# First attention of a two-layer graph transformer: the order of its loads and stores on the SyncE queue

## The reference

```python
x0 = layernorm(x)
for l in range(2):
    q = ((x0 @ Wq[l].T + bq[l]) * scaling).reshape(n, H, DH)
    k = (x0 @ Wk[l].T).reshape(n, H, DH)
    v = (x0 @ Wv[l].T).reshape(n, H, DH)
    scores = einsum('ehd,ehd->eh', q[tgt], k[srcidx])       # one score per edge and head
    w = softmax of scores over the edges that end in one node
    agg = segment_sum(w[:, :, None] * v[srcidx], tgt)
    x0 = batchnorm(x0 + agg @ Wo[l].T + bo[l])
    x0 = batchnorm(x0 + relu(x0 @ W1[l].T + b1[l]) @ W2[l].T + b2[l])
x = x + layernorm(x0)
x = x + small three-way MLP on decoded features of layernorm(x)
```

## Time and profile before

| | us |
|---|---|
| runs: median of 3 (lowest, highest) | 1113.53 (1112.64, 1302.58) |
| the profiled execution, its own time | 1110.29 |
| its span, first to last instruction | 1108.5 |
| PE busy in it | 1024.0 (92%) |
| DVE busy | 763.8 (69%) |
| ACT busy | 597.0 (54%) |
| POOL busy | 304.4 (27%) |
| PE waiting in the key jobs of layer 0 for VectorE | 3.67 |
| PE waiting in the first attention for `q_stack` | 3.61 |

### The profile page before, as it was taken

How to read it: one execution, slowest core, us unless ns; L and a number is a source line. 1 busy time by engine, 2 the same in 40 slices (tenths; PEclk the granted TensorE clock), 3 DMA queues, 4 the chain that set the end, 5 groups by cost and what they waited for, 6 DMA issues and landing times. The chain is left out here.

```text
span 1108.5 us, 18755 instructions
## 1 busy us (share of the span) xinstructions
PE 1024.0 (92%) x6579; PEld 852.7 (77%) x6579; DVE 763.8 (69%) x2350; ACT 597.0 (54%) x1096; POOL 304.4 (27%) x312
## 2 busy tenths in 40 slices
PE   4899899987999999999899999899999999989853
PEld 3678777876888888888699889788888888869842
DVE  6777647556777777777488730577777777747787
ACT  6633322435666666666425542566666666652366
POOL 1000000004444444443022200244444444421404
PEclk9999999999999999999999999999999999999985
DMA  6042310758112112113302454731211211320403
GB/s 146 24 158 79 116 46 23 165 136 217 41 35 58 38 38 62 38 38 112 114 1 99 105 127 102 179 65 38 61 38 38 62 38 39 112 86 1 94 4 93
DMA packets 50718, 84.98 MB, mean 77 GB/s; under 512 B 15190, under 2 KB 33466, under 8 KB 50372
## 3 DMA queue, kind: packets, MB, share of 16 engines
q1 hardware_dynamic: 50628, 83.82, 30.2%
HBM read 36.50 MB, written 21.61 MB: 52 GB/s over the span
## 5 line engine op out<-in xcount | busy, mean ns | idle before, releaser
L1259 POOL TENSOR_SCALAR probs<-probs,mass_inv 125x1250 f32<-125x1250 f32 x160 | 210.6, 1316 | 341.8 <-DVE mass_inv L1384 341.8
L1375 DVE CUSTOM_DVE_ANT_0 probs<-banks,scores_bias 125x416 f32<-125x416 f32 (+1 forms) x480 | 267.2, 582 | 49.6 <-PE banks L1279 45.2
L1279 PE MATMUL banks<-k_stack,q_stack 128*125 128x416 f32 (+1 forms) x960 | 294.7, 392 | 5.8 <-DMA q_stack<-q_split 3.6
L1293 PE MATMUL banks<-ident,probs 125*125 125x125 f32 x1600 | 258.6, 276 | 8.1 <-DVE probs_t L1366 5.8
L1293 PEld LDWEIGHTS banks<-ident,probs 125*125 125x125 f32 x1600 | 240.4, 187 | 32.0 <-issue 22.3
L1345 ACT ACTIVATE probs<-probs,neg_peak 125x1250 f32<-125x1250 f32 x160 | 213.4, 1334 | 54.4 <-DVE neg_peak L1398 54.4
L1334 ACT ACTIVATE probs_t<-banks 125x500 f32<-125x500 f32 x320 | 152.3, 477 | 111.9 <-PE banks L1293 111.9
L1308 PE MATMUL banks<-probs_t,v_pair 125*64 125x250 f32 x1600 | 186.2, 379 | 0.9 <-ACT probs_t L1334 0.9
L1279 PEld LDWEIGHTS banks<-k_stack,q_stack 128*125 128x125 f32 x960 | 143.8, 188 | 34.1 <-issue 15.9
L1308 PEld LDWEIGHTS banks<-probs_t,v_pair 125*64 125x64 f32 x1600 | 107.5, 136 | 54.3 <-ACT probs_t L1334 1.3
L1366 DVE COPY probs_t<-banks 125x500 f32<-125x500 f32 x160 | 108.1, 675 | 54.6 <-PE banks L1293 54.6
(11 more groups left out here) (256 smaller groups left out, 1410.3 us busy)
## 6 DMA issues: line engine op xcount, KB each, us to landing
q_stack<-q_split SPq DMA_DIRECT2D x160, 125.0 KB, 2.3
scores_bias<-edge_bias SPq DMA_DIRECT2D x8, 1171.9 KB
edge_bias<-bias_row SPq DMA_DIRECT2D x10, 585.9 KB
k_stack<-k_lo SPq DMA_DIRECT2D x16, 312.5 KB, 4.3
resid<-residual SPq DMA_DIRECT2D x2, 2500.0 KB, 9.7
values<-v_stage SPq DMA_DIRECT2D x2, 2400.0 KB
residual<-t SPq DMA_DIRECT2D x4, 625.0 KB, 3.0
xs<-in_x SPq DMA_DIRECT2D x5, 480.0 KB
```

The lines of the kernel that those rows point to most:

```text
L1259: nc.gpsimd.tensor_scalar(probs[:, u % 4, :], probs[:, u % 4, :], mass_inv[:, u % 4:u % 4 + 1], 1.0, ALU.mult, ALU.mult).then_inc(att["pro ...
L1279: mm = nc.tensor.matmul(pb[0:NT, t % 5, 0:sn], q_stack[:, n % 2, half, part, tile * NT:(tile + 1) * NT], k_stack[:, head * N + s0:head * N ...
L1293: mm = nc.tensor.transpose(pb[0:NT, 5 + t % 2, j * NT:(j + 1) * NT], probs[:, u % 4, (j0 + j) * NT:(j0 + j + 1) * NT], ident[0:NT, 0:NT])
L1375: nc.vector.tensor_tensor_reduce(out=probs[:, slot % 4, s0:s0 + sn], in0=pb[0:NT, t % 5, 0:sn], in1=scores_bias[:, (n % GROUPS) * GROUP + ...
```

## The change

It reorders what SyncE issues around the start of the first attention. `next_bias` is parted in `second_bias` (row 3) and `third_bias` (rows 4 and 5), and `values_out` in two parts, tiles 0 to 2 and tiles 3 to 9, with a semaphore each. In the first layer the store of the last bias row now stands right behind `first_bias`, ahead of the loads of rows 3 to 5; `k_stacked` of chunks 0 and 1 stand ahead of the queries of pass 1, with row 3 between them; rows 4 and 5 and the first part of the values are issued in the attention block. In both layers `stacked(2)` stands ahead of the load of rows 6 and 7, `stacked(3)` ahead of rows 8 and 9, and SyncE waits for the values ahead of `stacked(5)` instead of `stacked(4)`. ScalarE waits for the first part of the values before result 0 and for the second before result 5. No instruction of TensorE, VectorE, ScalarE or GpSimd is added, taken away or moved.

```diff
--- before.py
+++ after.py
@@ -240,7 +240,7 @@
 
         proj = {k: sem("p_" + k) for k in ("wq", "wv", "vec", "bias_q", "filled", "hi", "done", "copied")}
         k_stored = [sem("k_stored0"), sem("k_stored1")]
-        v_stored = sem("v_stored")
+        v_stored = [sem("v_stored0"), sem("v_stored1")]
         bias_in = [sem(f"bias_in{g}") for g in range(GROUPS)]
         v_in = [sem("v_in0"), sem("v_in1")]
         q_in = [sem("q_in0"), sem("q_in1")]
@@ -401,10 +401,14 @@
                 cols = slice((2 * c + half) * N, (2 * c + half + 1) * N)
                 sp.dma_start(f32(k_stack[other, cols]), f32(k_lo[c % 2][own, :])).then_inc(k_stored[c % 2], 16)
 
-        def values_out(sp):
+        V_PARTS = (slice(0, 3), slice(3, TILES))
+
+        def values_out(sp, k):
+
+            tiles = V_PARTS[k]
 
             for rows in SPREAD:
-                sp.dma_start(v_d.rearrange("(t p) d -> p t d", p=NT)[rows, :, :], v_stage[rows, :, :]).then_inc(v_stored, 16)
+                sp.dma_start(v_d.rearrange("(t p) d -> p t d", p=NT)[rows, tiles, :], v_stage[rows, tiles, :]).then_inc(v_stored[k], 16)
 
         def first_bias(sp):
 
@@ -414,11 +418,15 @@
             for rows in SPREAD:
                 sp.dma_start(scores_bias[rows, GROUP:GROUP + 1, :], bv[rows, GROUP:GROUP + 1, :]).then_inc(bias_in[1], 16)
 
-        def next_bias(sp):
+        def second_bias(sp):
 
             bv = bias_d.rearrange("(t p) s -> p t s", p=NT)
             for rows in SPREAD:
                 sp.dma_start(scores_bias[rows, GROUP + 1:2 * GROUP, :], bv[rows, GROUP + 1:2 * GROUP, :]).then_inc(bias_in[1], 16)
+
+        def third_bias(sp):
+
+            bv = bias_d.rearrange("(t p) s -> p t s", p=NT)
             for rows in SPREAD:
                 sp.dma_start(scores_bias[rows, 2 * GROUP:3 * GROUP, :], bv[rows, 2 * GROUP:3 * GROUP, :]).then_inc(bias_in[2], 16)
 
@@ -589,11 +597,13 @@
                 sp.wait_ge(bias_stored[0], 32 * (TILES // 2))
                 sp.wait_ge(bias_stored[1], 32 * (TILES // 2 - 1))
                 first_bias(sp)
-                next_bias(sp)
                 bias_out(TILES - 1)
-                for n in range(2):
-                    stacked(sp, n)
-                for c in range(DC - 1):
+                stacked(sp, 0)
+                k_stacked(sp, 0, 0)
+                second_bias(sp)
+                k_stacked(sp, 0, 1)
+                stacked(sp, 1)
+                for c in range(2, DC - 1):
                     k_stacked(sp, 0, c)
 
             @block.gpsimd
@@ -1230,16 +1240,21 @@
                     bv = bias_d.rearrange("(t p) s -> p t s", p=NT)
                     if layer == 0:
                         k_stacked(sp, 0, DC - 1)
-                        values_out(sp)
+                        third_bias(sp)
+                        values_out(sp, 0)
+                    stacked(sp, 2)
                     for k in range(2):
                         sp.wait_ge(k_stored[k], 32 * (DC // 2))
                     bias_part(3 * GROUP, 4 * GROUP)
-                    stacked(sp, 2)
+                    stacked(sp, 3)
                     bias_part(4 * GROUP, 5 * GROUP)
-                    stacked(sp, 3)
                     clear(sp, [*proj.values(), wk_in, res_stored])
-                    sp.wait_ge(v_stored, 32)
-                    for n in range(4, PASSES):
+                    stacked(sp, 4)
+                    if layer == 0:
+                        values_out(sp, 1)
+                    sp.wait_ge(v_stored[0], 32)
+                    sp.wait_ge(v_stored[1], 32)
+                    for n in range(5, PASSES):
                         stacked(sp, n)
                         c, g = divmod(n, GROUPS)
                         if c >= 1 and c + 1 < PAIRS and g == GROUPS - 2:
@@ -1335,7 +1350,9 @@
 
                     def out_of(n):
                         if n == 0:
-                            act.wait_ge(v_stored, 32)
+                            act.wait_ge(v_stored[0], 32)
+                        if n == GROUPS:
+                            act.wait_ge(v_stored[1], 32)
                         act.wait_ge(att["o_ready"], n + 1)
                         c, g = divmod(n, GROUPS)
                         nc.scalar.activation(attn[:, c, g * GN:(g + 1) * GN], pb[:, 7, 0:GN], ACT.Copy).then_inc(att["o_free"], 1)
@@ -1439,7 +1456,7 @@
             with nc.Block(no_gpsimd_drain=True) as block:
                 @block.sync
                 def _(sp):
-                    clear(sp, [*att.values(), *bias_in, *v_in, *q_in, v_stored, *k_stored])
+                    clear(sp, [*att.values(), *bias_in, *v_in, *q_in, *v_stored, *k_stored])
 
                     one = lambda v: v.rearrange("(a n) -> a n", a=1)
                     if last_layer:
```

## The result

The changed kernel took 1102.36 us in the median of 5 runs (1101.34 to 1105.30), the kernel before 1113.41 (5 runs, 1112.64 to 1302.58; the one of 1302.58 is a slow run, and the ratio leaves it out). The ratio is 0.9901, interval 0.9886 to 0.9916: 1.0% faster, a gain of 11.05 us where 9.2 were forecast. By the 2% bound that counts as the same; the interval, 9.4 to 12.7 us, shows a gain all the same. The profiled execution took 1102.37, its span is 1100.6.

The account below looks back on a forecast made before the run. The prediction took TensorE as the bound, with waits behind a full DMA queue. Gains of 5.5 + 3.7 = 9.2 us, taken from the median of 1113.53, gave 1104.3 us; range 1100.5 to 1109.5.

Parts of the forecast that it names:

- two terms: The gains forecast on TensorE: 5.5 us in the key jobs and 3.7 us at slot 8 of the first attention.
- Store ahead of rows 3 to 5: Before the key jobs: the last bias row's store meets an idle queue and lands 4.1 us after issue, not 9.87.
- What it is worth: Key jobs: TensorE's stop and the slow matmuls after it go, a gain of 5.5 us, bounds 0 to 5.5.
- Keys ahead of the queries of pass 1, row 3 between: Key jobs: second queries land near 234, wanted after 249; cost nothing, cover 15 us.
- Next in line: Key jobs after the stop: later banks are free, key copies land in 4.3 us, covered by 7 us.
- Slot 8: First attention: TensorE's 3.61 us wait for queries of pass 2 goes; gain 3.7 us, bounds 0 to 3.7.
- third rival: The clock falls at the other stop or at neither: 1105.9 us, or 1102.7 with a like price at slot 8; chance 0.12.
- The rest: Remaining order: later rows, values and queries land in time, cost nothing; nothing is put on layer 1.
- Rival 2: Slot 8 still waits since rows 4 and 5 replace the values; only 5.5 us go, 1108.0 us; chance 0.06.

Follow-up runs that it names:

- b4: The changed kernel with rows 3 and 4 loaded ahead of the last bias row's store, row 5 where rows 4 and 5 stood: 1102.56 us, ratio 0.9897.
- a1: The kernel before, unedited, timed and profiled a second time: 1113.68 us, ratio 0.9998.
- a3: The kernel before with queries of pass 2 ahead of rows 6 and 7, of pass 3 ahead of rows 8 and 9: 1108.58 us, ratio 0.9950.
- d1: The kernel before with the values stored in two parts, one right behind the other in the old place: 1111.36 us, ratio 0.9987.
- a2: The kernel before with only the last bias row's store moved ahead of the loads of rows 3 to 5: 1116.70 us, ratio 1.0022.
- a4: The kernel before with the edits of a2 and a3 together, values whole: 1110.26 us, ratio 0.9958.
- b2: The changed kernel with the second queries back ahead of the keys of chunks 0 and 1: 1101.74 us, ratio 0.9902.
- c1: The changed kernel with both parts of the values stored ahead of the queries of pass 2: 1101.52 us, ratio 0.9886.
- d2: c1 with the values stored in one piece, still behind rows 4 and 5: 1103.12 us, ratio 0.9904.

## Why the prediction was right, point by point

- **Sign, size and place: right.** Forecast 1104.3, measured 1102.36, in the range. In the profiles the two terms read 5.4 and 3.7 against 5.5 and 3.7.
- **Store ahead of rows 3 to 5.** Price taken 4.1 us from issue to landing, measured 4.60; the margin of two us covered that. With something queued right behind, queries or rows, it was 4.55 to 4.83 us in every kernel with at most four rows ahead. The 4.1 was read from SyncE, which waited for the store, the 4.60 from VectorE, so the half us is not shown to come from what stands behind. b4 shows where the margin ends.
- **What it is worth.** 5.5 us came from one execution. A was 32.09 to 33.83 in the four profiles of kernels with the old key part (before, a1, a3, d1), and 27.1 whenever the stop was gone, so 5.0 to 6.7 us. The clock behind the stop is one reason: in a3 it was at 0.50 to 0.57 from 226 to 232 us, in the first profile of the kernel before at 0.50 and 0.65 from 228 to 232.
- **"Keys ahead of the queries of pass 1, row 3 between. Cost nothing": the step that was wrong in its account.** The number was right for the whole change, by luck and not by the reasoning: I credited all 5.5 us to the early store and none to the placing of rows 3 to 5. a2 shows that the store alone makes the kernel 2.5 us slower and a4 that it takes 1.7 away from a3. What I did not follow was the chain from queries 0 over GpSimd's split and the second queries to the keys. In the changed kernel that chain has no rows ahead of it, and so the move of the keys cost nothing; b2 shows that it gained nothing either.
- **Next in line.** VectorE waited 1.34 and 2.15 us for its `k_lo` buffers, as late keys would have it (landing 5.1 us after the issue, 4.3 taken), and neither reached TensorE.
- **Slot 8: right in kind, small in size, and with half of the reason.** The forecast had the wait go because 1.15 MB fewer stand ahead. a3 had 3.2 MB ahead and no wait, as bytes would have it, but c1 had the full 4.45 MB and no wait either; the order of rows and values on the queue counts for more (c1, d1, d2). In size, 3.7 us is the stop without its clock. The third rival, that the clock may fall there too, is what the second profile of before shows: 4.8 us. The gain of a3, 5.7 us, lies nearer to that than to 3.7. This and the spread of A can make up what the gain of 11.05 has above 9.2 (6.7 and 4.8 would be 11.5); that the typical execution pays both is argued from single profiles and not shown. I had given it a chance of 0.12 shared with its opposite; it should have been a term.
- **Where to start from.** The first profile of before was an easy execution (1110.29 against medians from 1113.4 to 1114.25). I forecast against the median. From that execution it would have been 1101.1, nearer to the measured time (1.3 us under, where 1104.3 is 1.9 over), but by luck, by two errors that cancel: a start 3.1 us below the median and a gain 1.9 us too small.
- **The rest.** SyncE waited 1.6 us for the values ahead of `stacked(5)`, issued at 295.09, and nobody waited for it, as forecast. From the first score of layer 1 to its slot 7 are 720.85 - 694.77 = 26.08 us, 26.07 before. Rival 2 was out: a copy of queries took 2.4 us in the median in the changed kernel and the last was issued by 254.66 + 2.38 = 257.04, so they landed near 259 (an estimate from these), 7 us ahead of slot 8 near 243.81 + 22.65 = 266.5, and in c1 they were in time with 4.45 MB ahead as well. Storing most of the values later, which I took for a part of that cover, was not needed (c1).

## What to carry to other kernels

When DMAs share one in-order issuer, follow the whole chain through the engines that prepare each transfer before you price a move: here an earlier store alone made the kernel slower, since it pushed loads in front of small copies on which the next issue hung. Put bulk loads whose data are wanted late behind the small transfers that somebody waits for. A stop of a few us on TensorE can be worth more than the wait in the list (4.8 us for 3.8 in a1; 3.7 for 3.6 in the first profile): look in several executions for a stretch of low clock behind it.

## What the runs showed that I had not expected

- After stops of much the same length, 3.6 and 3.8 us at slot 8, the granted clock stayed at 1.00 in one execution and fell to 0.75 and 0.83 in two stretches of 4 us in another; the price was 3.7 and 4.8 us. The Trainium skill (TensorE: Matmul & The Clock Gate, on the HAM clock gate) has the point of the switch vary from run to run. It says so of the rise under load; here it is the fall that came in one profile of a kernel and not in the other.
- With the same bytes, the time in which the queue drained differed by up to 4.9 us (26.3 against 21.4) by the order of loads and stores on it and by how the store is cut. A full queue is no measure of its rate: in the profile of c1 alone, stretches of 2 us with the DMA engines busy for 0.96 to 1.00 of the time moved 141 GB/s (269 to 271 us) and 387 GB/s (255 to 257 us).
